# Expert 0's rows without the last tile's, which come by products with one-hot rows; scatters and a tile's routing moved

## The reference

```python
def _L0_xattn_ref(...):            # per tile of tokens
    out = jnp.einsum('bnf,fd->bnd', out, Wout)
    out = (out - mu) * jax.lax.rsqrt(var + EPS) * ln_scale + ln_bias
def _L0_ffn_ref(inputs, Wr, br, W1, b1, W2, b2):
    x = inputs.reshape(B * T, D)
    C = N // E                      # 512 slots for each expert
    logits = x @ Wr + br
    gate, idx = max and argmax of softmax(logits)
    pos = (jnp.cumsum(mask, axis=0) * mask).astype(jnp.int32)
    mask = mask * (pos < C)         # later tokens of a full expert are dropped
    expert_in = jnp.einsum('nd,nec->ecd', x, dispatch)   # rows times gate
    h = jax.nn.relu(expert_in @ W1 + b1)
    eo = h @ W2 + b2
    out = eo back to the tokens, times gate
```

## Time and profile before

| | |
|---|---|
| median of 3 runs | 1337.8 us (1336.18 to 1341.15) |
| the profiled execution | 1337.9 us |
| its span in the trace | 1336.1 us |
| PE busy | 1294.8 us, 97% |
| DVE, ACT, POOL busy | 935.6, 659.8, 412.9 us |
| from the last warming after the output product to expert 0's first product | 1117.4 to 1138.4 us of the span |

### The profile page before, as it was taken

The page is one execution under the profiler, slowest core; times in us unless marked ns, Lnnn a source line. Parts: engine busy times, 40 slices in busy tenths (PEclk is TensorE's granted clock), DMA queues, the critical chain, the costliest instruction groups (busy, mean ns, idle before and its releaser), DMA issues.

```text
span 1336.1 us, 31436 instructions
## 1 busy us (share of the span) xinstructions
PE 1294.8 (97%) x12285; PEld 1054.4 (79%) x12285; DVE 935.6 (70%) x1872; ACT 659.8 (49%) x1837; POOL 412.9 (31%) x476
## 2 busy tenths in 40 slices
PE   7999899999999999999999999999999998999998
PEld 7988667777777778888888888888888875788886
DVE  6549678887786666777777777776766786565663
ACT  4447333333333755555556555555555661565552
POOL 2213445445432011212231231312212213546453
PEclk9999999999999999999999999999999998999999
DMA  8962142222322201103021020110102103555530
GB/s 260 327 217 64 57 152 80 88 91 86 112 92 99 79 9 41 51 14 110 10 73 48 17 104 17 60 60 17 65 24 95 57 17 133 185 185 176 168 110 22
DMA packets 68656, 122.69 MB, mean 92 GB/s; under 512 B 12249, under 2 KB 20465, under 8 KB 68514
## 3 DMA queue, kind: packets, MB, share of 16 engines
q1 hardware_dynamic: 60194, 97.11, 21.8%
q0 software_dynamic: 8320, 23.62, 5.1%
HBM read 82.13 MB, written 42.07 MB: 93 GB/s over the span
## 4 chain that ended last, share of the span: by engine, by line
PE 84%; DVE 10%; ACT 3%; issue 2%; DMA 1%; POOL 1%; SPq 0%; DVEq 0%; POOLq 0%
PE bank L70 19%; PE bank L72 18%; PE bank L71 17%; PE bank L2161 6%; PE bank L2149 5%; PE bank L2182 4%; PE bank L2174 2%; PE bank L2269 2%; PE bank L1232 2%; PE bank L1262 2%; PE bank L1206 1%; ACT b_prob L1549 1%; PE bank L2222 1%; PE bank L2660 1%; PE bank L2233 1%
## 5 line engine op out<-in xcount | busy, mean ns | idle before, releaser
L1549 ACT ACTIVATE b_prob<-bank,b_neg_top 128x155 f32<-128x155 f32 x496 | 187.3, 407 | 118.6 <-DVE b_neg_top L1741 110.7
L70 PE MATMUL bank<-turned_h,big_h 128*128 128x512 f32 x320 | 130.6, 408 | 1.8 <-DVE turned_l L1936 1.5
L72 PE MATMUL bank<-turned_h,big_l 128*128 128x512 f32 x320 | 125.5, 392 | 0.0
L71 PE MATMUL bank<-turned_l,big_h 128*128 128x512 f32 x320 | 124.9, 390 | 0.0
L1741 DVE TENSOR_REDUCE b_neg_top<-bank 128x6 f32<-128x930 f32 (+1 forms) x93 | 94.3, 1014 | 28.8 <-PE bank L2161 28.7
L70 PE MATMUL bank<-b_wo_h,b_ot_h 128*128 128x512 f32 x256 | 112.7, 440 | 0.4 <-DVE b_ot_l L1770 0.4
L2149 PEld LDWEIGHTS bank<-ident,b_prob 128*128 128x128 f32 x640 | 93.2, 191 | 24.5 <-DVE b_pt L1758 8.6
L2149 PE MATMUL bank<-ident,b_prob 128*128 128x128 f32 x640 | 103.1, 283 | 5.6 <-DVE b_pt L1758 4.8
L1549 ACT ACTIVATION_READ_ACCUMULATOR b_prob<-bank,b_neg_top 128x1 f32 x496 | 102.7, 207 | 0.0
L72 PE MATMUL bank<-b_wo_h,b_ot_l 128*128 128x512 f32 x256 | 101.2, 396 | 0.0
L1752 DVE TENSOR_TENSOR b_prob<-b_prob,b_recip 128x930 f32<-128x930 f32 (+1 forms) x93 | 98.4, 1058 | 3.4 <-DVE b_recip L1749 0.2
(11 more groups left out here) (315 smaller groups left out, 3362.0 us busy)
## 6 DMA issues: line engine op xcount, KB each, us to landing
wide<-in_L_ffn_W_dram SPq DMA_DIRECT2D x16, 1024.0 KB, 5.5
slot_rows<-empty_row SPq DMA_DIRECT2D x8, 1032.0 KB, 13.8
a_xr<-in_x_dram SPq DMA_DIRECT2D x32, 256.0 KB, 2.7
x_scratch<-a_xr SPq DMA_DIRECT2D x32, 256.0 KB, 2.1
tiles<-x_scratch SPq DMA_DIRECT2D x32, 256.0 KB, 3.9
rows<-x_scratch SPq DMA_DIRECT2D x32, 256.0 KB, 3.6
out_dram<-rows SPq DMA_DIRECT2D x32, 256.0 KB, 2.0
rows<-slot_rows SPq DMA_DIRECT2D x7, 1032.0 KB, 8.5
```

The source lines that it names most:

```text
L70: pe.matmul(out, lh, rh, start=first, stop=False)
L71: pe.matmul(out, lh, rl, start=False, stop=False)
L72: return pe.matmul(out, ll, rh, start=False, stop=last)
L1549: last = act.activation(prob[:, n % 2, j, h:h + 2 * L2 - 1:2], s_banks[:, h, o:o + L2], ACT.Exp, bias=neg_top[:, n % 2, h, j:j + 1], accum ...
```

## The change

Expert 0's rows are fetched twice. The first fetch (four pieces, into the same place) is issued when the tiles up to 30 are scattered; the last tile's rows may be missing from it. These come in another way: ACT norms tile 31's own rows where they lie (`mine`), DVE compares the numbers 0 to 511 with each token's slot (`picked`, a one-hot row for each token, all zero for a token that belongs to another expert), and eight products of `mine`'s two parts with `picked` place the turned rows in four banks. The fetched rows, normed on ACT, are added there by sixteen products with the identity, no longer transposes, since they accumulate; the slots that the last tile fills are still empty in them. The banks are now divided by features and not by tokens, and the first layer of expert 0 starts as soon as the first of four is split, its first two steps interleaved. The last scatter waits until the first fetch has landed. The second fetch, which brings gates, token numbers and the rows that are added at the end, is issued after it; the biases of expert 0 are scaled by it and so move behind the third and the fourth relu.

To this come: tiles 28 to 30 routed in one go (`route_apart`) before the norm of tile 31; the scatters of tiles 24 to 27 ahead of two powers on POOL, those of tile 28 ahead of the power of tile 31 and of 29 and 30 behind it; one warming product instead of eight; the negated mean times the factor kept in a row in place of the mean, which is one more DVE step in each batch; and a different order of the output product, the turn and the logits on PE.

```diff
     BATCHES = [(G * g, G) for g in range(NG - 1)] + [(NT - G, G - 1), (NT - 1, 1)]
-    BASE = [sum(20 + c for _, c in BATCHES[:r]) for r in range(len(BATCHES))]
-    TOPS, CHOSEN, READY = 2, 6, 13
...
+    STEPS = [21 + c for _, c in BATCHES[:LAST - 1]] + [23, 16]
+    BASE = [sum(STEPS[:r]) for r in range(len(BATCHES))]
+    TOPS, CHOSEN, READY = 2, 6, 14
...
+        sp.wait_ge(s["scattered"], SENT[LAST])
+        for k in range(G):
+            sp.dma_start(rows[:, 0, k, :], slot_tiles[:, k, :]).then_inc(first_rows[k], 16)
...
             if n == NT - 1:
+                hold(pool, s["s_done"], NS * (NT - 1))
+                pool.iota(numbers_i[:, :], pattern=[[1, CAP]], base=-T, channel_multiplier=0)\
+                    .then_inc(s["numbered"], 1)
+                scatter(i - 1)
+                power("w", n)
                 power("y", n - 1)
+            elif n == NT:
+                power("y", n - 1)
+                scatter(LAST - 1, 0, 1)
                 power("w", n)
-                scatter(i - 1)
+                scatter(LAST - 1, 1)
+                return
...
             if n == NT + 1:
-                scatter(LAST - 1)
+                for k in range(G):
+                    hold(pool, first_rows[k], 16)
                 scatter(LAST)
-                pool.sem_inc(s["scatter_issued"], 1)
...
+                need(act, s["route_step"], BASE[LAST] + 10)
+                spare = rows[:, (NT - 1) // G % 2, (NT - 1) % G, :]
+                act.activation(mine[:, :], spare[:, 0:D], ACT.Identity, bias=spare[:, D + 2:D + 3],
+                               scale=spare[:, D + 3:D + 4]).then_inc(s["mine_normed"], 1)
+                need(act, s["mine_normed"], 1)
+                act.activation(mine_h[:, :], mine[:, :], ACT.Copy).then_inc(s["mine_high"], 1)
                 for k in range(G):
+                    act.wait_ge(first_rows[k], 16)
+                    act.activation(xn[:, k, :], rows[:, 0, k, 0:D], ACT.Identity, bias=rows[:, 0, k, D + 2:D + 3],
+                                   scale=rows[:, 0, k, D + 3:D + 4]).then_inc(s["first_normed"], 1)
+                for k in range(KD):
                     need(act, s["first_turned"], k + 1)
-                    act.activation(xt_h[:, :, k * P:(k + 1) * P],
-                                   first_banks[k].rearrange("p (k t) -> p k t", k=KD), ACT.Copy)\
-                        .then_inc(s["first_high"], 1)
+                    act.activation(xt_h[:, k, :], first_banks[k], ACT.Copy).then_inc(s["first_high"], 1)
...
                 lambda: dve.tensor_tensor(put(D + 3), rstd["y"][:, k], gate, ALU.mult),
+                lambda: dve.scalar_tensor_tensor(put(D + 2), put(D + 2), -1.0, put(D + 3), ALU.mult, ALU.mult),
...
+        def route_apart(r):
...
+            router(BASE[r], [
+                lambda: dve.tensor_scalar(put(D + 1, G).bitcast(I32), token_int[:, every], 0, None, ALU.add),
+                lambda: dve.tensor_scalar(c4["slot4"][:, :], token_f[:, every], -1.0, float(CAP * E - T), ALU.mult,
+                                          ALU.add),
+            ])
+            logits(NT - 2)
...
+                lambda: dve.tensor_reduce(top4, lg, AX.X, ALU.max),
+                lambda: dve.tensor_tensor(q_e[:, k, :], lg, by8(top4, c), ALU.subtract),
...
+                lambda: dve.scalar_tensor_tensor(slot, rank4, -float(CAP), slot, ALU.mult, ALU.add),
...
+        def add_counts(r):
...
+            router(BASE[r] + 22, [
+                lambda: dve.tensor_tensor(before[:, 0, :], before[:, c - 1, :], tot[:, c - 1, :], ALU.add),
...
         def route_last():
...
                 lambda: dve.scalar_tensor_tensor(slot, pos, float(CAP), slot, ALU.is_lt, ALU.mult),
+            ])
+            need(dve, s["route_step"], BASE[LAST] + 14)
+            dve.tensor_scalar(picked[:, :], numbers[:, :], spare, slot, ALU.subtract, ALU.is_equal).then_inc(s["placed"], 1)
+            need(dve, s["mine_high"], 1)
+            dve.tensor_tensor(mine_l[:, :], mine[:, :], mine_h[:, :].bitcast(F32), ALU.subtract).then_inc(s["mine_low"], 1)
...
             if n == NT:
                 need(dve, s["x2_made"], n - 1)
                 norm_stats("y", n - 1, row(n - 2), EPS1)
-                logits(n - 2)
-                route_tops(LAST - 1)
-                route_gates(LAST - 1)
+                route_apart(LAST - 1)
                 w_stats(n - 1)
                 add_residual(n - 1)
                 need(dve, s["x2_made"], n)
                 norm_stats("y", n, row(n - 1), EPS1)
-                route_slots(LAST - 1)
+                add_counts(LAST - 1)
                 logits(n - 1)
                 route_last()
-                need(dve, s["scatter_issued"], 1)
                 for k in range(4, 8):
                     expert_split(k)
-                for k in range(G - 1):
-                    first_norm(k)
-                first_rest(0)
-                first_norm(G - 1)
-                for k in range(1, G):
...
+            if n == NT - 1:
+                need(dve, s["numbered"], 1)
+                dve.tensor_copy(numbers[:, :], numbers_i[:, :]).then_inc(s["numbered"], 1)
...
         def warm(count):
+            need(pe, s["s_exp"], NS * (NT - 1))
+            for _ in range(count):
+                pe.matmul(s_banks[:, 0, :], ident[:, :], lns_b[:, :], start=True, stop=True)
...
+        def first_turns():
...
             need(pe, s["ot_low"], 2 * NT)
-            for _ in range(count):
-                pe.matmul(ot_bank[1], ident[:, :], lns_b[:, :], start=True, stop=True)
+            need(pe, s["placed"], 1)
+            for half, part, ready in ((0, mine_h, s["mine_high"]), (1, mine_l, s["mine_low"])):
+                need(pe, ready, 1)
+                for c in range(KD):
+                    pe.matmul(first_banks[c], part[:, c * P:(c + 1) * P], picked[:, :], start=half == 0, stop=False,
+                              skip_group_check=True)
+            for k in range(G):
+                need(pe, s["first_normed"], k + 1)
+                for c in range(KD):
+                    last = pe.matmul(first_banks[c][:, k * P:(k + 1) * P], xn[:, k, c * P:(c + 1) * P], ident[:, :],
+                                     start=False, stop=True, skip_group_check=True)
+                    if k == G - 1:
+                        last.then_inc(s["first_turned"], 1)
...
         def step(i, t, n):
             if n == NT:
+                turn_y(n - 2)
                 output(n - 1, 0, 2)
-                turn_y(n - 2)
+                logits(n - 2)
                 output(n - 1, 2, 4)
-                logits(n - 2)
-                output(n - 1, 4, 6)
-                output(n - 1, 6, 8)
+                output(n - 1, 4, 5)
                 count(LAST - 1)
+                output(n - 1, 5, 8)
                 warm(3)
                 turn_y(n - 1)
                 logits(n - 1)
                 count_last()
-                warm(8)
-                need(pe, s["s_exp"], NS * (NT - 1))
-                need(pe, s["w_evac"], NT)
-                need(pe, s["q_evac"], KI * (NG - 1))
-                for k in range(G):
-                    need(pe, s["first_normed"], k + 1)
-                    for c in range(KD):
-                        last = pe.transpose(first_banks[k][:, c * P:(c + 1) * P], xn[:, k, c * P:(c + 1) * P],
-                                            ident[:, :])
-                    last.then_inc(s["first_turned"], 1)
+                warm(1)
+                first_turns()
...
             sp.wait_ge(late["scattered"], late["sent"])
+            sp.wait_ge(late["first_normed"], G)
             for k in range(G):
                 sp.dma_start(rows[:, 0, k, :], slot_tiles[:, k, :]).then_inc(late["first_rows"][k], 16)
...
-            act.wait_ge(late["first_rows"][k], 16)
+            act.wait_ge(late["first_rows"][k], 32)
...
         def prepare(e, par):
-            hold(act, s[f"b_loaded{par}"], 32)
-            for k in range(G):
-                first_bias(k)
+            pass
...
                 act.activation(ht_h[:, c, :], h[:, c % 2, :], ACT.Copy).then_inc(s["h_high"], 1)
                 if c == 1 and more:
                     weights(e + 1, 1 - par, 0)
+                if isinstance(e, int) and e == 0 and c >= 2:
+                    first_bias(2 * c - 4)
+                    first_bias(2 * c - 3)
...
+            if isinstance(e, int) and e == 0:
+                for k in range(G):
+                    dve.wait_ge(late["first_rows"][k], 32)
+                tail(e, par)
...
         def work(e, par, more):
             if isinstance(e, int) and e == 0:
-                pe.wait_ge(late["expert_low"], 8)
-                pe.wait_ge(late["first_low"], G)
+                pe.wait_ge(late["expert_low"], 4)
+                for c, k in ((0, 0), (1, 0), (0, 1), (1, 1), (0, 2), (0, 3), (1, 2), (1, 3)):
+                    pe.wait_ge(late["first_low"], k + 1)
```

(6 more changed lines are left out.)

120 lines of the change are left out of this document (82 added, 38 removed).

## The result

| | before | changed |
|---|---|---|
| median of 15 runs | 1337.8 us | 1343.29 us |
| lowest to highest | 1334.84 to 1341.5 | 1339.11 to 1346.43 |
| changed / before, 95% interval | | 1.0040 (1.0027 to 1.0053) |
| profiled execution, its span | 1337.9, 1336.1 | 1345.04, 1343.3 |

The prediction was 1334.8 us in a range of 1331.5 to 1338.8. The prediction had held changes under 0.5% to be no change, and 5.5 us are 0.4%; but the interval lies clear of 1, on the side of slower, and the time is out of the range.

What follows compares the result with a forecast made beforehand. PE's 23.9 us gap before expert 0's first product, released by DMA, was the bound. First product 4.6 us earlier, fourth part 3.3 us earlier after a weight wait, less 0.2: 1334.8 us, range 1331.5 to 1338.8.

Steps and rivals of the forecast that it cites:

- Routing and scatters: POOL and DVE ahead of the last tile: residual add moves by 0.5 us, PE's output products by 0.3 us.
- the late power: POOL's w variance power, behind four scatters ending at 1105.15: DVE's residual add 0.5 us later, PE's output products 0.3.
- Routing of the last tile, one-hot rows, products: Last tile's chain: starts 1121.3, fourteen steps end 1124.4, one-hot rows 1124.95, expert 0's first product 1133.85, 4.6 us earlier.
- Expert 0's rows: Early fetch, issued when tile 30's scatter lands at 1122.2: pieces land from 1124.8 to 1127.2, ACT's norms end at 1127.9.
- the sum: Whole forecast: fourth part at 1148.45 against 1151.77, 3.3 us earlier, less 0.2 us for late copies, giving 1334.8 us.
- tile 30's scatter: Scatter ahead of the first fetch: starts at about 1118.9, lands 3.28 us later at 1122.2.
- What comes due instead: Expert 1's first weight, queued behind the second fetch, lands at 1141.9; ACT waits 1.0 us, fourth part at 1148.45.
- The counting point: Start of the fourth part of expert 0's second layer, 1151.77 before: gain counted there, 3.3 us, less 0.2.
- the two bias scalings between the relus: On ACT, between expert 0's third and fourth relu: 2.55/4 us each, ending at 1146.3.
- (a): Rival: PE's clock stays low from 1124.9 on, fourth part at 1153.7, kernel 1340.0 us; chance 0.08.
- (d): Rival: tile 30's scatter held behind a POOL power, or fetches 3 us late; last scatter and weight slide; 1337.8 us; chance 0.07.
- The clock's rule: PE's clock: low after little work, high after 6.1 us of unbroken products; taken as low from 1123 until about 1130.1.

Runs made afterwards that it cites:

- e7: Kernel before, with only POOL's scatters of tiles 24 to 27 put ahead of the w and y variance powers: 1340.34 us, ratio 1.0018.
- e1: Changed kernel with POOL's old order restored, y and w powers ahead of the scatters of tiles 24 to 27: 1340.29 us, ratio 1.0021.
- e8: Changed kernel plus 14 unused products in PE's two waits of expert 0's second layer: 1339.83 us, ratio 1.0024.
- e16: Kernel before, with only expert 0's four bias scalings on ACT moved behind the third and fourth relu: ratio 1.0020.
- e15: e12 without POOL's eight adds of the residual rows for experts 0 and 1: ratio 0.9975.
- e10: e1 plus expert 1's first weight issued before the second fetch, third rest ahead of expert 1's norms, bias scalings behind the fourth relu: ratio 1.0013.
- e12: e10 plus five warming products in the waits of the last tile's chain on PE: 1338.49 us, ratio 0.9999.
- e13: e12 with two rests and results ahead of the weight's rest on DVE, two row copies ahead of expert 1's scalings on ACT: ratio 0.9973.

## Why the prediction was wrong, step by step

**Routing and scatters: the step that failed first.** I gave the late power 0.5 us on DVE and 0.3 on PE. The power itself was about right: it started 0.5 us later against the mark than predicted (four scatters took 5.3 us, not 4.85). Wrong was what I let it cost. Behind it in POOL's queue stands an add of 128x512, which before ran at 1110.27, long after the residual add, and now beside it: 2.21 us for 0.81. PE stood still for 2.53 us, and the clock fell for the products behind; PE's new order isn't needed for that, since it waited 2.43 us in e7 without it. The warming behind the output products starts 3.7 us later against the mark, not 0.3. e7 shows the edit's cost by itself, e1 its removal.

**Routing of the last tile, one-hot rows, products.** Right, within 0.6 us each. From the start of that warming to the chain's first step it took 7.02 us (6.45 predicted), its fourteen steps and the compare 3.67 (3.65), from the one-hot rows to the first product 8.54 (8.90). The sixteen true fp32 products took 3.90 us, 0.24 each (0.25 predicted for the high clock). The number filling and its cast were free.

**Expert 0's rows.** The early fetch works, but took 6.0 us to land (1127.92 to 1133.93), not 5.0, and POOL started the last scatter 0.84 us behind that, where I had 0.1. The first fetch itself was issued 0.5 us later against the first product than in the sum. So the last scatter came 4.3 us ahead of the first product, not 6.55. POOL's order isn't the cause of this: in e1, where it is undone, it is 4.4 us. What the sum had too early there is tile 30's scatter, put 19.2 us behind the mark without a working; it was 21.4 in e1 and 23.2 in the changed kernel.

**What comes due instead: right mechanism, wrong size.** I named the weight behind the last scatter as what holds ACT. Its landing was 11.7 us behind the second fetch's issue (11.3 predicted). The wait was 3.33 us, not 1.0, and nearly all of the 2.3 us more are the 2.2 us by which the scatter was nearer to the first product. This makes up 2.3 of the 2.8 us by which the stretch to the fourth part was longer than predicted. The rest is near the 0.6 us by which the fourth rest was slower than in the sum: 1.32 us, beside POOL's adds, and not 0.69. The two stops of 1.80 and 2.13 us then also took the clock down, behind the fourth part.

**The counting point: the other step that failed.** I wrote that behind the fourth part nothing has a stall that the change removes, and allowed 0.2 us for one that it brings. It was 2.46. With the clock kept high 1.1 of it go (e8), and PE waits 1.27 us for DVE instead. As far as the traces tell, that wait is the copy of the gates: the change moves it behind the fourth rest, beside POOL's adds, where it takes 1.25 us; e16 has the slow rest of the weight in the same place, but not this copy, and no such wait. That the adds slow DVE down is shown (e15); their share in the changed kernel was not tested by itself. I priced the two bias scalings between the relus on ACT, and not POOL's adds that follow from them; the rows of the kernel before that show them in DVE's quiet stretch were there to be read. e10 is the sharpest case: in its trace it reaches the counting point 50.39 us behind the mark, 1.7 us sooner than the kernel before (52.11), and it is 4.2 us later at the end.

By stretches the miss of 8.7 us is 3.6 before the first product, 2.8 from there to the fourth part, and 2.3 behind it. The rivals: (a), the low clock, had a time near (1340.0) for another place; (d) let the last scatter slide by 3 us and the weight with it. Against the mark it came 5.9 us later than in the sum, but a power on POOL is not what held tile 30's scatter: POOL had waited 7.50 us for the slots of tiles 28 to 30. And I had let (d) end at 1337.8, as if a late start could cost no more than the gain.

The clock's rule, weighed in the prediction as what might keep PE slow in the last tile's chain: the granted clock was low there from 1128 to 1134, the cost that the sum held. That broken work also takes the clock down elsewhere is what the rows above show, at 1110.9 and at 1156. By the Trainium skill, page "TensorE: Matmul & The Clock Gate", section on the HAM clock gate, the throttled state is the default that only sustained activity leaves; the traces agree in that the clock is at 0.50 behind these stops, though in e12 it stayed at 1.00 behind one of 3.18 us.

## What to carry to other kernels

Price a step that is moved by what its whole queue does around the new place: the instruction behind it, and the work that follows from it on a third engine. Put the counting point behind the last place that the change touches by such a consequence, not at the first place where the old kernel is dense again. A transfer taken out of one wait belongs to a queue: what is put behind it (here expert 1's rows, then the norms, then the rests) is due next, and each may need its own move before the gain is seen; here the moves of e13 together turned +0.4% into -0.3%. And read the clock in both traces before a stretch is compared: behind the same wait the same code took 2.6 us longer in e10, where the clock fell, than in e12, where it didn't.
